# Gates multiplied into the weights of the out-projections, and rows of constants requested earlier

## The reference

```python
# layer L0 (L2 and L3 are alike; some of their branches have no gate or no bias)
x = x + g_self  * (self_attention(norm(x) ...)      @ w_so + b_so)
x = x + g_cross * (cross_attention(norm(x), context) @ w_co + b_co)
x = x + g_mlp   * (mlp(norm(x) ...)                 @ w_m2 + b_m2)
```

## Time and profile before

| | |
|---|---|
| three timed runs | 2862.53, 2864.98, 2874.17 us; median 2864.98 us |
| the profiled execution's own time | 2869.71 us |
| its span (first to last instruction) | 2868.4 us |
| mean granted clock of PE | 0.912 of full speed |
| PE busy | 2420.5 us (84%) |
| DVE busy | 1745.0 us (61%) |
| POOL busy | 375.5 us (13%) |

### The profile page before, as it was taken

One profiled execution on the slowest core, in us unless ns is written; L12 is line 12 of the kernel. 1 busy time (PEld: TensorE's weight loads), 2 busy tenths in 40 slices (PEclk: granted clock), 3 DMA queues, 4 the chain that ended last, 5 costly groups with the idle time before them and its releaser, 6 DMA issues.

```text
span 2868.4 us, 37341 instructions
## 1 busy us (share of the span) xinstructions
PE 2420.5 (84%) x13127; PEld 1239.4 (43%) x13127; DVE 1745.0 (61%) x5419; ACT 1264.1 (44%) x2410; POOL 375.5 (13%) x380
## 2 busy tenths in 40 slices
PE   6768677968997979999979999978889978899668
PEld 2455344544554544554434445432324332234335
DVE  5646856666234565557767666657676677775343
ACT  2324434433221314445525555525656626656334
POOL 3002333244010100000200010010010010010201
PEclk9889688989898979999989999989999989999879
DMA  4646231000000120000411100123110122110120
GB/s 157 170 118 201 89 114 32 17 24 6 3 8 30 67 61 12 12 23 26 143 59 57 36 16 23 45 88 98 50 32 12 67 81 75 31 26 8 55 60 15
DMA packets 151647, 161.32 MB, mean 56 GB/s; under 512 B 33471, under 2 KB 120978, under 8 KB 151196
## 3 DMA queue, kind: packets, MB, share of 16 engines
q1 hardware_dynamic: 151460, 158.94, 19.2%
HBM read 98.04 MB, written 60.19 MB: 55 GB/s over the span
## 4 chain that ended last, share of the span: by engine, by line
PE 62%; DVE 16%; issue 6%; ACT 5%; DMA 5%; POOL 4%; SPq 2%; POOLq 0%; ACTq 0%; DVEq 0%
PE bank L1125 9%; PE bank L1608 8%; PE bank L1097 7%; PE bank L1072 7%; PE bank L1629 5%; PE bank L736 3%; PE bank L1101 3%; PE bank L2082 3%; DVE max L1198 3%; DVE bank L1195 2%; PE bank L1528 2%; PE bank L2259 2%; PE bank L2084 1%; PE bank L676 1%; ACT work L1139 1%
## 5 line engine op out<-in xcount | busy, mean ns | idle before, releaser
L1139 ACT ACTIVATE work<-bank 128x512 f32<-128x512 f32 (+1 forms) x1216 | 700.7, 597 | 574.6 <-PE bank L1101 259.4
L1195 DVE CUSTOM_DVE_ANT_0 bank<-bank,weights 128x512 f32<-128x512 f32 x512 | 348.8, 703 | 197.8 <-PE bank L1072 196.4
L1198 DVE TENSOR_REDUCE max<-bank 128x1 f32<-128x512 f32 x512 | 341.3, 685 | 142.4 <-PE bank L1072 140.4
L1072 PE MATMUL bank<-k_stack,q_stack 97*128 97x512 bf16 x896 | 364.4, 410 | 70.5 <-DVE max L1198 28.6
L1097 PE MATMUL bank<-q_stack,k_stack 99*128 99x512 bf16 x896 | 345.4, 388 | 12.8 <-ACT work L1139 10.3
L1608 PE MATMUL bank<-hT,weights 128*128 128x512 f32 x512 | 268.3, 624 | 16.0 <-ACT hT L697 7.4
L1453 POOL TENSOR_TENSOR x<-x,work 128x512 f32<-128x512 f32 x64 | 82.1, 1282 | 1081.3 <-DVE work L1442 1076.9
L1101 PEld LDWEIGHTS bank<-ident_b,weights 128*128 128x128 bf16 x2048 | 159.3, 98 | 119.3 <-issue 10.3
L1072 PEld LDWEIGHTS bank<-k_stack,q_stack 97*128 97x128 bf16 x896 | 90.1, 101 | 267.8 <-DVE max L1198 99.3
L1101 PE MATMUL bank<-ident_b,weights 128*128 128x128 bf16 x2048 | 200.1, 220 | 0.0
L1629 PE MATMUL bank<-weights,work 128*128 128x256 f32 x768 | 196.5, 384 | 0.0
(11 more groups left out here) (237 smaller groups left out, 3687.2 us busy)
## 6 DMA issues: line engine op xcount, KB each, us to landing
q_stack<-parts_q SPq DMA_DIRECT2D x60, 384.0 KB, 3.9
parts_q<-parts SPq DMA_DIRECT2D x46, 384.0 KB, 2.6
k_stack<-parts_k SPq DMA_DIRECT2D x40, 384.0 KB, 4.8
weights<-parts_q SPq DMA_DIRECT2D x36, 384.0 KB, 3.7
parts_q<-parts SPq DMA_DIRECT2D x46, 256.0 KB, 2.9
parts_k<-parts SPq DMA_DIRECT2D x24, 384.0 KB, 2.5
parts_k<-parts SPq DMA_DIRECT2D x24, 256.0 KB, 2.9
weights<-in_L_e_w SPq DMA_DIRECT2D x12, 512.0 KB, 5.8
```

The lines of the kernel that those rows point to most:

```text
L1072: m = pe.e.matmul(bank.ap[:, :], self.q(g)[0:MAX_ROW, h, qt * P:(qt + 1) * P], k_stacks[self.key, g].ap[0:MAX_ROW, h, half * BLK:(half + 1 ...
L1139: ac.e.activation(p.ap[0:self.nk, :], banks[self.key, "exp", g, i].ap[0:self.nk, :], ACT.Exp).then_inc(*probs.tick((self.key, g, i)))
L1195: ve.e.tensor_tensor_reduce(bank[:, :], bank[:, :], mask_bias[:, qt, half * BLK:(half + 1) * BLK], 1.0, -3.4e38, ALU.add, ALU.max, to).the ...
L1198: ve.e.tensor_reduce(to, bank[:, :], AX_X, ALU.max).then_inc(*maxima.tick((self.key, g, i)))
```

## The change

Four things are changed together.

1. **Gate in the weights.** For a gated out-projection POOL multiplies the weights (128 x 2 x 256) by the gate row once (new line L1503, into one of two new buffers `gated0`, `gated1`; 12 products, since two stages share one), and PE reads those in place of `weights`. DVE adds the bank straight into `x` (the `direct` branch of `add_vector`, formerly for the ungated case only), and POOL's adds for these stages, 40 of the 64 at L1453, are gone, as are the 40 multiplications of DVE at L1442. The MLPs keep both. PE's matmuls of the projection now wait for the product, which waits for the rows and the weights; DVE's add waits for the bias adds of POOL where there is a bias, else for the norm's `z`.
2. **Rows requested earlier.** The row buffer of an out-projection is free once its product (and its bias adds) are done. `Mlp.sync` is gone and an explicit `early` stands in front of each MLP. The rows of the L2 `so` of batch 0 and 1 and of the L3 `so` are requested at the end of the phase before the one that uses them.
3. **The last phase shares its rows.** The two lanes of batch 1 have one set of rows: `co` in buffer 0, `so` and `mlp` in buffer 1, one gated product and one product of bias and gate for both.
4. **`k_rows2` moved** from the start of phase 6 to behind the MLP of batch 1's first half.

```diff
         class Adding(Stage):
+            shared = None
+            def rows_key(self):
+                return (self.shared or self).key
...
             def pre_add(self, po):
...
                 if self.gate is not None:
-                    po.e.tensor_tensor(tmc[r][:, 1, :], tmc[r][:, 1, :], tmc[r][:, 0, :], ALU.mult).then_inc(
...
+                    if self.shared is None:
...
+                        po.e.tensor_tensor(tmc[r][:, 1, :], tmc[r][:, 1, :], tmc[r][:, 0, :], ALU.mult).then_inc(
             def added(self, t):
-                return (pool_done if self.gate is not None else vec)[self.key, "x", t - t % 2]
+                return (vec if self.direct else pool_done)[self.key, "x", t - t % 2]
             def add_vector(self, ve, tp, bank, y):
-                if self.gate is None:
+                if self.direct:
                     if self.bias is not None:
                         ve.wait_ge(*pool_done[self.key, "pre", tp + 1])
+                    else:
+                        ve.wait_ge(*vec[self.norm.key, "z", tp + 1])
                     ve.e.tensor_tensor(x[b][:, tp:tp + 2, :], x[b][:, tp:tp + 2, :], src, ALU.add)...
         class OutProject(Adding):
+            direct = True
             def pool(self, po):
+                if self.gate is not None and self.shared is None:
+                    w = gated.take(self.r, self.key, (dense, (self.key, "all")))
+                    for f in w.free:
+                        po.wait_ge(*f)
+                    po.wait_ge(*ld_w[self.wname][self.wname])
+                    po.wait_ge(*ld_tm[self.r][self.key, "rows"])
+                    po.wait_ge(*pool_done.latest)
+                    po.e.tensor_tensor(w.ap[:, :, :], wt[self.wname][:, :, :], tmc[self.r][:, 0:1, :].to_broadcast([P, CC, C]),
+                                       ALU.mult).then_inc(*pool_done.tick((self.key, "gated")))
                 self.pre_add(po)
                 yield
-                for what, tp, i in self.steps:
-                    yield
-                    if what == "pair" and i == 1 and self.gate is not None:
-                        self.add_pool(po, tp, work[self.key, "y", tp])
             def project(self, pe, bank, tile, i):
                 w = wt[self.wname]
+                if self.gate is not None:
+                    w = gated[self.rows_key()].ap
+                    pe.wait_ge(*pool_done[self.rows_key(), "gated"])
         class Mlp(Adding):
+            direct = False
-            def sync(self, sp):
-                self.load_rows(sp)
-                yield
...
-            ([k_rows2] + of(1, ("co", 0), ("n3", 0), ("mlp", 0)) + [early(1, ("co", 1))] + of(1, ("co", 1), ("n3", 1), ("mlp", 1)),
+            (of(1, ("co", 0), ("n3", 0)) + [early(1, ("mlp", 0))] + of(1, ("mlp", 0)) + [k_rows2] + [early(1, ("co", 1))] + of(1, ("co", 1), ("n3", 1)) + [early(1, ("mlp", 1))] + of(1, ("mlp", 1)),
...
-            (of(1, "self3"), [rows_0] + last_0),
-            ([rows_10] + last_10, [rows_11] + last_11),
+            (of(1, "self3"), last_0 + [rows_co] + end_0[:2] + [rows_mlp] + end_0[2:3] + [rows_so1] + end_0[3:]),
+            ([rows_co1] + last_10 + [rows_mlp1] + end_10, last_11),
```

More of the change, by code:

```diff
@@ L283, in build_program @@
         eb2 = sb("e_b2", [E, C])
+        gated = slots([sb(f"gated{i}", [P, CC, C]) for i in range(2)])
         stats = [sb(f"stats{b}", [P, NT, 6]) for b in range(B)]
@@ L1424, in rows_left @@
                 if self.gate is not None:
-                    left.append((vec, (self.key, "y", self.tiles[-1] - 1)))
+                    left.append((pool_done, (self.rows_key(), "gated")) if self.direct else (vec, (self.key, "y", self.tiles[-1] - 1)))
                 if self.bias is not None:
@@ L1440, in add_vector @@
                     ve.wait_ge(*f)
-                ve.wait_ge(*ld_tm[r][self.key, "rows"])
+                ve.wait_ge(*ld_tm[r][self.rows_key(), "rows"])
                 ve.e.tensor_tensor(y.ap[:, :].rearrange("p (t f) -> p t f", t=2), src, tmc[r][:, 0:1, :].to_broadcast([P, 2, C]),
@@ L1512, in tensor @@
                             bank = banks.take(self.lane.banks[n % len(self.lane.banks)], k, (vec, (self.key, "y", at)))
-                            work.take(self.lane.work[4 + n % 4], (self.key, "y", at), (pool_done, (self.key, "x", at))
-                                      ) if self.gate is not None else None
                             for f in bank.free:
@@ L1520, in tensor @@
                             m.then_inc(*dense.tick(k))
+                            dense.also((self.key, "all"), k)
                             n += 1
@@ L1550, in vector @@
                         ve.wait_ge(*dense[self.key, tp])
-                        self.add_vector(ve, tp, banks[self.key, tp], work[self.key, "y", tp] if self.gate is not None else None)
+                        self.add_vector(ve, tp, banks[self.key, tp], None)
                     yield
         class Mlp(Adding):
+            direct = False
             def __init__(self, lane, b, name, norm, gated_unit, gate, bias, row_free, blk=None, r=None):
@@ L2589, in build_program, with last_stages @@
                            [[(pv_sums, (S_[b]["cross2"].key, 7, "all"))] for b in range(B)], False, True)
-        def last_stages(b, blk, lane, r, rows, slots_at, ones, cross):
+        def last_stages(b, blk, lane, r, rows, slots_at, ones, cross, shared=None):
             st, last = S_[b], NB - 1 if blk is None else blk
-            so = OutProject(lane, b, "L3so", "L3so", st["self3"], st["n7"], ("L3", 2 * C), a["L3_b_proj"], rows, blk=blk, r=r)
-            rows = so.rows_left()
+            so = OutProject(lane, b, "L3so", "L3so", st["self3"], st["n7"], ("L3", 2 * C), a["L3_b_proj"], rows[r], blk=blk, r=r)
             n8 = Norm(lane, b, "L3n2", 1e-6, one, zero, None, so.added, [(turned, (so.key, "all"))], blk=blk)
@@ L2600, in last_stages @@
                               rows_ready=ones, keys_ready=context3.keys(b), blk=blk, **cross)
[L2601 to L2602 removed]
+            co = OutProject(lane, b, "L3co", "L3co", cross, n8, None, a["L3_b_cproj"], rows[0], blk=blk, r=0)
             n9 = Norm(lane, b, "L3n3", 1e-6, modulation("L3", 8, b), modulation("L3", 6, b), ("L3", "norm", 2), co.added,
                       [(turned, (co.key, "all"))], blk=blk)
[L2605 removed]
@@ L2606, in last_stages @@
-            return Rows(so), [so, n8, xq, cross, Rows(co), co, n9, mlp, Store(b, mlp)], mlp.rows_left()
-        xq_ones, q_ones = [("xq_rows", 0), ("xq_rows", 1)], [("q_rows", 0), ("q_rows", 1)]
-        rows_0, last_0, rows = last_stages(0, None, lane_d, 0, S_[0]["rows3"], (0, 1), xq_ones, cross_of)
-        rows_10, last_10, _ = last_stages(1, 0, lane_a, 0, rows, (2, 3), q_ones, dict(cross_of, max_banks=(0, 1), exp_banks=(2, 3), pv_banks=(4,)))
-        rows_11, last_11, _ = last_stages(1, 1, lane_d, 1, S_[1]["rows3"], (0, 1), xq_ones, cross_of)
+            mlp = Mlp(lane, b, "L3", n9, False, ("L3", 5 * C), a["L3_b_mlp2"], [], blk=blk, r=r)
@@ new lines, in last_stages @@
+            if r == 0:
+                co.row_free = so.rows_left()
+            mlp.row_free = (co if r == 0 else so).rows_left()
+            if shared is None:
+                return Rows(so), Rows(co), Rows(mlp), [so, n8, xq, cross], [co, n9, mlp, Store(b, mlp)], (so, co, mlp)
+            for stage, other in zip((so, co, mlp), shared):
+                stage.shared = other
+            shared[2].row_free = shared[2].row_free + so.rows_left()
+            return [so, n8, xq, cross, co, n9, mlp, Store(b, mlp)]
```

30 lines of the change are left out of this document (16 added, 14 removed).

## The result

The changed kernel is slower: ratio 1.005 to the kernel before, 95% interval 1.0029 to 1.007. Medians of six executions each: 2886.7 us (2877.8 to 2894.6) against 2868.9 us. The forecast was 0.40% faster. The profiled execution of the changed kernel took 2879.09 us, span 2877.8, which is 9.4 us over the span of before; it is one of the fastest of its six, so the trace shows a part of the loss and not all of it.

The account below looks back on a forecast made before the run. PE was taken to bound the kernel (busy 84% of the span). The terms 5.9 − 7.0 + 3.5 + 3.0 + 4.4 + 1.5 = 11.3 us led to a forecast of 2853.5 us (−0.40%), range 2842 to 2867.

Parts of the forecast that it names:

- Phase 6, first half: Start of phase 6: memsets gone from ahead of the bias product, norm's last z earlier; gain 5.9 us (2.6 to 7.3).
- Second half: Phase 6, second half: PE waits 7.45 us for the gated product behind the moved memsets; loss 7.0 us (4.5 to 7.45).
- At the others I take 0: Gated product at the 12 places: late at only one, in phase 6; price 0 elsewhere (0 to 1.3 us each).
- Phase 10: Start of phase 10: L2 `so` row requested 14 us earlier, PE's wait goes; gain 3.5 us (0 to 4.4).
- Phase 11: Start of phase 11: rows requested 4.4 us earlier, DVE's wait goes; gain 3.0 us (0 to 4.4).
- Rival 2: Phases 10 and 11: DVE takes the gains back or rows still land late; sum 4.8, time 2860 us; chance 0.18.
- Last phase: Last phase: statistics no longer wait for POOL's four adds, PE's 13.83 us idling shrinks; gain 4.4 us (3.0 to 5.3).
- Phase 4: Top-k search: POOL's first step no longer waits behind an add that waits for DVE; gain 1.5 us (0 to 3).
- DVE's part: Gated out-projections: DVE's 40 multiplications become 40 additions into x of equal time, 0.69 us; cost 0.
- The chances: Whole kernel: faster (under 2850.7 us) 0.38, no difference 0.54, slower (over 2879.3 us) 0.08.
- Rival 3: After PE's 7.45 us stall in phase 6, some 28 us at half clock cost 14 us; time 2868; chance 0.13.
- Rival 1: Start of phase 6: shorter PE idle avoids the clock drop, 5.5 us more gain; sum 16.8, time 2848; chance 0.27.

Follow-up runs that it names:

- e5: Kernel before with only the changed kernel's interleave of PE, DVE and ACT, made with empty beats; rows, weights and adds as before: ratio 1.007.
- e1: Changed kernel with its lanes' beats put back, so PE, DVE and ACT keep the order of the kernel before: ratio 0.9983 to the kernel before.
- e10: As e1, but L0's cross-attention projections ungated as before and the memsets inside the first MLP of phase 6: ratio 0.9957 to the kernel before.
- e2: As e1, with the four memsets behind everything else of POOL in phase 6: ratio 0.9983 to the kernel before.
- e7: As e1, with the memsets behind the first cross-attention projection of phase 6: ratio 0.9957 to the kernel before.
- e3: Kernel before with only the early rows, shared in the last phase; no gated weights, memsets at the start of phase 6, order as before: ratio 0.9957.
- e4: As e1, but L0's four cross-attention projections ungated as before and the memsets at the start of phase 6: ratio 0.9953 to the kernel before.
- e6: Kernel before with only the gated weights; rows where they were except the last phase's shared set, memsets at phase 6's start, order as before: ratio 1.0051.
- e11: Kernel before with the shifted interleave in phases 5 and 6 alone: ratio 1.0016.
- e12: Kernel before with the shifted interleave from phase 8 on, phases 0 to 7 in the order of before: ratio 1.0062.

## Why the prediction was wrong

**The step that failed** is one that the prediction never writes down. It goes "through the timeline at each place where an out-projection begins" and counts what stands there as if the rest of the program kept its order. The line of the diff that adds a beat was read as an earlier request only. Its price, the interleave of PE, DVE and ACT from phase 5 on, is 1.007 alone (e5) and as large as the whole distance between the changed kernel (1.005) and e1 (0.9983).

With the order restored, the change wins 0.17% by time (0.05 to 0.3) instead of the 0.40% forecast. That e1's profile lies 10.3 us below before's, close to the sum of 11.3, is luck: the execution was a fast one, and the terms of the sum account for only 4.1 − 7.9 + 2.5 + 2.5 + 6.2 = 7.4 us of it. The largest of the steps outside them is −3.6 from 1400 to 1700, where kernels with the same order scatter from −4.0 to +1.8.

By its terms, measured with the order restored (e1, steps from 685 on):

- Phase 6, first half: 5.9 forecast, 4.1 found. Mechanism half right: e10 shows 5.2 by 735 and 6.2 by 760 without the gate, so the gated product took 1 to 2 of what the memsets' absence gave.
- Second half: 7.0 loss forecast, 7.9 found, the wait 7.66 for 7.45. The memsets are 5.5 of it; the other 2.1 are the late row that e2 and e7 still have, which the prediction took as there in time.
- **At the others I take 0**: right in e1 (0.33 us), wrong in the changed kernel for 2.73, where the weave put the projection closer behind the row's request. Of the 5.95 only 0.3 are the product's; the rest is the weave's wait for ACT (5.41 in e5).
- Phase 10: 3.5 forecast; 2.5 in e1, 5.1 in e3, 4.8 in e4. Phase 11: 3.0 forecast; 2.5, 3.7, 3.7. The early rows did this, with the gate in the weights or without. **Rival 2** (given back by DVE) falls for phase 11. For phase 10 it is right in part: from 1960 to 2280 the eight kernels with early rows and the weave of before lose 0.4 to 3.2 us again (e1 the 3.2, all of its gain), while of the four with late rows e6, e11 and e12 don't (−1.1, −0.1, −0.9) and e5 does (2.0). That DVE takes it back isn't shown.
- Last phase: 4.4 forecast, 6.2 in e1; 3.2 in e3 and 3.7 in e4, PE's idling 9.44 and 9.04 for the "near 9" forecast. The size is right and the cause wrong: it was put down to POOL's adds of `y`, and nearly all of it is there with these adds in place, by the early, shared rows. The prediction had the rows ready "from before the `Store`" without a price for their lateness before.
- Phase 4: 1.5 forecast, nothing found (−0.1 in e1 up to 385, within a scatter from −5.6 to +7.3 at this point between kernels that have the same order of PE, DVE and ACT).
- DVE's part, 0: right, L1445 takes 0.69 us.
- The chances: 0.14 + 0.85 × 0.27 is 0.37 and not 0.38, which changes nothing.

**Rival 3**, the clock, has the right place and the wrong size. The windows of the changed kernel around its wait of 7.66 us (us, PE busy, PEclk, DMA share, GB/s):

```profile
816.00:820.00 4.00, 0.00 (x0) 1.00 0.02 5
820.00:824.00 4.00, 0.34 (x1) 0.50 0.00 0
824.00:828.00 4.00, 4.00 (x13) 0.65 0.00 0
828.00:832.00 4.00, 4.00 (x17) 1.00 0.35 66
...
824.00:827.00 3.00, 3.00 (x8) 0.53 0.00 0
827.00:831.00 4.00, 4.00 (x19) 1.00 0.35 66
```

The clock did fall to 0.50, 1.2 GHz, during the idle, and was back at full from about 827 on, some 3 us after work began at 823.66: not after the 28 us of the earlier trace rows. At 0.65 of full over four busy microseconds that is 1.4 us of PE's work. The price of 14 us also took PE as busy throughout these 28 us of before, and it was busy for 12.45 of them:

```profile
706.00:734.00 28.00, 12.45 (x40) 0.54 0.03 10
```

**Rival 1**, a gain by the clock, did not come. The first half of phase 6 still ran at the lower level in the changed kernel, with its idle of 4.16 us in place of 6.83:

```profile
731.00:741.00 10.00, 9.92 (x33) 0.50 0.00 0
```

No rival named the weave, and "slower" had 0.08.

## What to carry to other kernels

Where a table of stages sets the interleave of in-order engines, every stage that is added or taken away is a change of order for all of them, even one that issues a single transfer: compare the order of the engine that bounds the kernel first, and hold it fixed while judging the rest. Moving a factor from behind a matmul to its weights moves the dependence on that factor from the engine behind to the one that bounds, so it pays only where the factor is there early, and the request for it has to be moved with it. A short helper on an idle engine (four memsets here) costs by what stands behind it in its queue and by what runs on DVE beside it; inside the long idle of an MLP the trace shows no cost. And where two edits are made together, a gain at the expected place and of the expected size (the last phase here) doesn't show which of them made it.

## What the runs showed of the hardware

- A memset of POOL (1.80 us) held DVE's tensor-scalar operations on 128x4 for up to its whole length, 1.45 to 1.82 us against 0.16 to 0.17, in three of three cases in e7. The norm's operations on 128x4 with two inputs ran beside the last of these memsets in 0.16 us. DVE's direct add with a bank as one input stayed within 672 to 689 ns in 48 cases, 12 of them beside POOL.
- In an idle of 7.66 us PE's clock fell to its lower level and was full again some 3 us after work began, in the changed kernel. In the first half of phase 6 it stayed low for longer: over 20 us before, with PE busy for less than half of the time, and in the changed kernel for 10 us in which PE was busy for 9.92. What makes the one return early and the other late was not tried.
- The first 385 us, where the transfers are densest (a DMA share of 0.50, and 0.09 to 0.20 in later stretches of the same length), differ by up to 13 us between profiles of kernels with the same order of PE, DVE and ACT. A single profile doesn't show a difference of 10 us in span as such; the step between two points of it shows more, to some 6 us: from 1400 to 1700 these kernels scatter from −4.0 to +1.8.
